# Eight scatters of a turn issued one by one behind the turn's matrix products, in the first graph layer

## The chip, the cores and the metric

The kernel runs on one core of a Trainium2 chip. The metric is the device time of one execution, in microseconds; lower is better. Times are given as the median of several executions, with the lowest and the highest beside it.

## The reference, cut to what matters

The program is a stack of four graph layers and four feed-forward layers over 32 graphs of 256 nodes with 128 features, all in float32. The change is in the first graph layer, which also prepares the routing of the first feed-forward layer:

```python
# layer 0, graph part, with h = layer norm of x
h1 = relu(bn1(conv1(h)));  h2 = bn2(conv17(h1));  x_conv = relu(h2 + h)
s = h @ w_se.T + b_se;     A = exp(-dist(s)) * mask
msg = relu(h @ w_msg.T + b_msg);  x_nmp = A @ msg
gi = [x_conv, x_nmp] @ w_ih.T + b_ih;  gh = h @ w_hh.T + b_hh
r = sigmoid(gi_r + gh_r);  z = sigmoid(gi_z + gh_z)
out = (1 - z) * tanh(gi_n + r * gh_n) + z * h;   x = x + out
# layer 0, feed-forward part: two of 16 experts for each row
logits = norm(x) @ gate_w + gate_b;  top_k(softmax(logits), 2)
y = sum over the two of gate * ((silu(row @ w1) * (row @ w2)) @ w3)
```

The reference computes every expert for every row; the kernel sorts the rows by expert first. Each normalised row is written twice, to a slot in the region of each of its two experts in a buffer in device memory called `sorted_rows`.

## The kernel before

**Turns.** The 8192 rows are worked in 16 turns of 512 rows (two graphs, four tiles of 128 rows). `every_turn` (line 38) writes turns 0, 1, 14 and 15 out and loops over the others in pairs. Each engine has its own program, whose order is written by hand; engines meet only at semaphores. `B[0]` to `B[7]` are the eight PSUM banks.

**TensorE in turn t** (lines 591 to 667), in this order, with the semaphore that each product raises: the first convolution (`c1_ps`), the distance features (`s_ps`), the messages (`msg_ps`), the ranks of turn t-2 for the router, convolution taps (line 607), the transposes of turn t-1's output (`out_ps`), the hidden state's product (`ghn_ps`, line 629), the distances (`dist_ps`, line 634), more taps with `shared_ps` and then `c2_ps` (line 642), the router's transposes of the normalised rows of turn t-1 (`hT_ps` of the route, line 1019), the transposes for turn t+1 (line 581), the neighbours' sum (`nmp_ps`, line 654), the router's logits of turn t-1 (`logits_ps`, line 1027), and the gate products (lines 661, 664, 667), of which the last three raise `r_ps`, `n_ps` and `z_ps`.

**The router's chain, for turn t-1, within turn t.** VectorE adds the residual and takes the row statistics (`vector_stats`, which ends with the variance on line 854, `var_ready`). GpSimd raises the variance to the power -0.5 (`pool_rstd`, line 966, `rstd_ready`). VectorE makes the shift (`vector_shift`, lines 859 and 861). ScalarE writes the normalised rows into `rows[par]` (`scalar_rows`, line 985, `h_ready`). TensorE transposes them (line 1019), ScalarE copies that out of PSUM (line 994), TensorE makes the logits (line 1027), and VectorE picks the two experts (lines 868 to 908). ScalarE's program has the copy of line 552 (`g_shared`) right behind the four copies of line 985; TensorE's line 654 waits for it. VectorE's normalisation of turn t+1 (line 185) is behind line 861.

**Places and scatters, for turn t-2, within turn t.** VectorE turns the ranks into slots (`vector_places`, line 940, `slots_ready`), ahead of the residual of turn t-1. GpSimd then issues eight scatters (`dispatch`, line 756): two experts times four tiles of 128 rows, each an indirect DMA of 128 rows of 528 bytes. There are two buffers of rows and slots, taken in turn; `vector_shift` waits until the scatters of a buffer have landed (two turns earlier) before it writes it again.

**GpSimd before** has nothing else in a turn: the power for t-1 first, then the eight scatters for t-2 in a row.

**SyncE** loads two 512 KB blocks of adjacency a turn, two turns ahead: the first once line 457 has used its buffer, the second after line 472. So turns 14 and 15 load nothing.

The same `Route` class serves two later layers; their GpSimd programs (lines 1560 to 1583 and 2990 to 3010) call `pool_dispatch`, as before.

Of the kernel before, what the change touches and what calls it, by code (L numbers as in the profile page):

```python
# [21 lines left out]
ALU = mybir.AluOpType  # L22
# [9 lines left out]
TT = TURN // P  # L32
# [5 lines left out]
def every_turn(eng, body, count=TURNS, begin=1):  # L38

    for t in range(begin + 1):  # L40
        body(t, t % 2, t == 0, False)
    with eng.Fori(begin + 1, count - 3, 2) as t:
        body(t, 0, False, False)
        body(t + 1, 1, False, False)
    body(count - 2, 0, False, False)
    body(count - 1, 1, False, True)
# [186 lines left out]
def wait_past(eng, sem, value):  # L233

    if not isinstance(value, int) or value > 0:
        eng.wait_ge(sem, value)


def counted(eng, value):

    return value if isinstance(value, int) else eng.to_reg(value)
# [9 lines left out]
def phase_gnn0(nc, c):  # L251
# [14 lines left out]
    with ExitStack() as ctx:  # L266
# [3 lines left out]
        def sem(name):  # L270
            return c.sem("g0_" + name)
# [38 lines left out]
        dist_ps, exp_ready, A_ready = sem("dist_ps"), sem("exp_ready"), sem("A_ready")  # L310
# [5 lines left out]
        c2_ps, xpre_ready, xconv_ready = sem("c2_ps"), sem("xpre_ready"), sem("xconv_ready")  # L316
        nmp_ps, nmp_ready = sem("nmp_ps"), sem("nmp_ready")
        ghn_ps, r_ps, z_ps, n_ps = sem("ghn_ps"), sem("r_ps"), sem("z_ps"), sem("n_ps")
# [5 lines left out]
        route = Route(nc, c, "ffn0", c.moe, ctx, B[2], B[2], B[2])  # L324

        with nc.Block() as block:
            @block.sync
            def _(sp):
                def load(t, par, first, last):
                    if not first and not (isinstance(t, int) and t == 1):  # L330
                        sp.wait_ge(A_ready, t - 1)
                    sp.dma_start(adj[par][:], c.adjT[t]).then_inc(adj_ready[par], 16)
                    if not first and not (isinstance(t, int) and t == 1):
                        sp.wait_ge(degrees_done, t - 1)
                    sp.dma_start(adj_rows[par][:], c.adj[t]).then_inc(adj_rows_ready[par], 16)
                    if isinstance(t, int) and t == 1:
                        nxt = c.order[1]
                        sp.dma_start(c.block[nxt], c.dram[nxt]).then_inc(c.w_ready[nxt], 16)
                every_turn(sp, load)

            @block.gpsimd
            def _(g):

                g.wait_ge(consts, 1)
                g.tensor_tensor(bnc[:, 6:8], bnc[:, 4:6], c.minus_half[:, 0:2], ALU.pow).then_inc(consts_pow, 1)
                route.pool_begin(g)

                def turn(t, par, first, last):
                    if first:
                        return  # L350
                    route.pool_rstd(g, t - 1)
                    if not (isinstance(t, int) and t == 1):
                        route.pool_dispatch(g, t - 2, par)
                every_turn(g, turn)
                route.pool_rstd(g, TURNS - 1)
                route.pool_dispatch(g, TURNS - 2, 0)
# [393 lines left out]
    r.dispatched = [c.dma_sem[name, "dispatched", i] for i in range(r.depth)]  # L750


def dispatch(eng, c, m, r, par):
    for k in range(m.top):
        for j in range(TT):
            eng.indirect_dma_start(c.sorted_rows, bass.IndirectOffsetOnAxis(r.slot[par][:, k, j:j + 1], 0),  # L756
                                   r.rows[par][:, j, :], None).then_inc(r.dispatched[par], 16)

# [6 lines left out]
class Route:  # L765
# [3 lines left out]
    def __init__(self, nc, c, name, r, ctx, rows_bank, logits_bank, rank_bank, in_phase=True):  # L769
        m, L = MOE[name], LAYOUT[name]  # L770
# [11 lines left out]
        def sem(n):  # L782
            return c.sem(f"{name}_r_{n}")
# [15 lines left out]
         self.logits_in, self.top_ready, self.shifted, self.first_eq, self.first_ready, self.hot_first, self.left_ready,  # L799
         self.second_top, self.second_eq, self.second_weighed, self.second_ready, self.hot_second, self.chosen_ready, self.exp_ready,  # L800
         self.den_ready, self.pair_sum, self.pair_eps, self.pair_inv, self.rank_ps, self.counted, self.used_ready,
         self.picked, self.slots_ready, self.inside_ready, self.kept_ready, self.routed) = (sem(n) for n in (
             "zeroed filled upto_ready merged squared joined rms var_ready "
             "rstd_ready shift_ready h_ready hT_ps hT_ready logits_ps "
             "logits_in top_ready shifted first_eq first_ready hot_first left_ready "
             "second_top second_eq second_weighed second_ready hot_second chosen_ready exp_ready "
             "den_ready pair_sum pair_eps pair_inv rank_ps counted used_ready "
             "picked slots_ready inside_ready kept_ready routed").split())
        self.scattered = r.dispatched

    def tiles_(self, ap):
        return ap[:, :, None].broadcast_to([P, TT, self.m.count])
# [155 lines left out]
    def pool_dispatch(self, g, t, par):  # L968
        done = counted(g, t + 1)
        g.wait_ge(self.zeroed, 2)  # L970
        g.wait_ge(self.slots_ready, done)
        g.wait_ge(self.h_ready, done)
        dispatch(g, self.c, self.m, self.r, par)

# [68 lines left out]
def moe_table(nc, c, name, m, w, r, nxt):  # L1045

    E, B = m.count, c.bank
    with ExitStack() as ctx:
# [19 lines left out]
        with nc.Block() as block:  # L1068
# [15 lines left out]
            @block.gpsimd  # L1084
            def _(g):
                dispatch(g, c, m, r, (TURNS - 1) % r.depth)
# [2496 lines left out]
```

## Time and profile before

| what | us |
|---|---|
| median of 3 executions (lowest to highest) | 3343.19 (3338.99 to 3350.63) |
| the profiled execution's own time | 3378.2 |
| its span, first to last instruction | 3376.4 |
| mean granted TensorE clock in it | 0.904 of full speed |
| busy in the span: PE, PEld, DVE, ACT, POOL | 2714.6, 2131.5, 2205.6, 1742.1, 872.7 |

PE is TensorE's matrix products and PEld its weight loads, DVE is VectorE, ACT is ScalarE, POOL is GpSimd. Work is named by line, engine, operation and tiles (out<-in). In a timeline each row has the start in the span, the time that it took, and in brackets how long its engine sat idle before it and what ended that. Starts of matrix products are recorded, their ends are modelled. "remote" stands where the semaphore moved at a time at which no instruction of the profile ended. The layer runs from the start to about 560 us; turn 2 starts near 92 us, turn 14 near 481.

### The profile page before, as it was taken

What the parts mean: (1) busy time and instruction counts of PE and PEld (TensorE: products, weight loads), DVE (VectorE), ACT (ScalarE), POOL (GpSimd) and SP (SyncE); (2) the same over time, 40 slices, a digit from 0 to 9 for tenths busy, and PEclk for the clock granted to TensorE, in tenths of its full rate; (3) what the DMA queues carried; (4) which work ended last, traced back from release to release, by engine and by line L of the source; (5) the groups of instructions that cost most, each with busy time, mean ns of one, the idle gap of its engine ahead of it and who ended that gap; (6) DMA issues with size and microseconds to landing.
All of it is one profiled execution on the core that took longest, in us unless ns stands there. A gap on an engine that the chain in (4) does not pass through costs nothing. (4 is left out here: it accounts for less than half of the span.)

```text
span 3376.4 us, 67489 instructions
## 1 busy us (share of the span) xinstructions
PE 2714.6 (80%) x19706; PEld 2131.5 (63%) x19706; DVE 2205.6 (65%) x6555; ACT 1742.1 (52%) x5034; POOL 872.7 (26%) x863
## 2 busy tenths in 40 slices
PE   5798995888677586578999998899987777669992
PEld 4566674877457585265777877566654444468882
DVE  5666664444467554767888885699986667644445
ACT  2233332444456453475656563677756666445553
POOL 0222332444425343230001010000001343434332
PEclk9899997999789798889999999899998888779996
DMA  5111111222332121320000000000010000022115
GB/s 195 42 46 48 57 45 47 67 63 65 117 123 76 50 58 47 126 79 1 1 1 0 0 1 10 26 19 25 19 34 37 21 24 20 26 59 56 53 53 165
DMA packets 142589, 169.06 MB, mean 50 GB/s; under 512 B 19920, under 2 KB 118224, under 8 KB 141776
## 3 DMA queue, kind: packets, MB, share of 16 engines
q1 hardware_dynamic: 116688, 118.67, 11.9%
q0 software_dynamic: 21504, 44.74, 3.9%
q10 hardware_dynamic: 4224, 3.59, 0.4%
q8 instruction: 79, 1.29, 0.2%
q14 instruction: 94, 0.77, 0.1%
HBM read 115.87 MB, written 51.05 MB: 49 GB/s over the span
## 5 line engine op out<-in xcount | busy, mean ns | idle before, releaser
L1375 PE MATMUL bank<-ffn_e_xT,ffn_e_mine 128*128 128x128 f32 x3360 | 462.8, 285 | 56.3 <-ACT ffn_e_mine L1309 24.4
L1233 POOL DMA_INDIRECT y_rows<-ffn_e_rows_out,ffn_e_scatter_at x352 | 339.0, 963 | 523.4 <-DVE ffn_e_rows_out L1261 331.6
L1375 PEld LDWEIGHTS bank<-ffn_e_xT,ffn_e_mine 128*128 128x128 f32 x3360 | 423.1, 199 | 68.0 <-issue 41.7
L756 POOL DMA_INDIRECT sorted_rows<-ffn_rows,ffn_slot x320 | 315.9, 987 | 231.2 <-issue 220.1
L1385 PE MATMUL bank<-ffn_e_mine,ffn_e_hid 128*128 128x128 f32 x1968 | 294.9, 283 | 39.1 <-DVE ffn_e_hid L1281 17.6
L1281 DVE TENSOR_TENSOR ffn_e_hid<-ffn_e_act,bank 128x256 f32<-128x256 f32 (+1 forms) x280 | 135.9, 485 | 276.3 <-ACT ffn_e_act L1335 245.1
L1309 ACT ACTIVATE ffn_e_mine<-constants 128x512 f32 (+1 forms) x352 | 250.9, 714 | 87.1 <-issue 64.4
L1385 PEld LDWEIGHTS bank<-ffn_e_mine,ffn_e_hid 128*128 128x128 f32 x1968 | 256.2, 196 | 55.9 <-DVE ffn_e_hid L1281 26.5
L2752 ACT ACTIVATE gnn_prob<-bank,gnn_low 128x256 f32<-128x256 f32 x512 | 203.0, 500 | 107.0 <-DVE gnn_low L2666 107.0
L1335 ACT ACTIVATE ffn_e_act<-bank 128x256 f32<-128x256 f32 (+1 forms) x280 | 120.8, 431 | 247.0 <-PE bank L1375 174.1
L1269 DVE TENSOR_SCALAR ffn_e_mine<-constants 128x256 f32 (+2 forms) x352 | 123.6, 354 | 119.6 <-PE bank L1385 73.0
L966 POOL TENSOR_TENSOR ffn_r_rstd<-ffn_r_var,minus_half 128x4 f32<-128x4 f32 x48 | 49.8, 1038 | 576.9 <-DVE ffn_r_var L854 405.7
L2666 DVE TENSOR_REDUCE gnn_low<-bank 128x2 f32<-128x512 f32 x256 | 158.9, 683 | 23.1 <-PE bank L2851 20.4
L2677 DVE SCALAR_TENSOR_TENSOR gnn_probT<-gnn_adj,bank 128x512 f32<-128x512 f32 x256 | 163.6, 680 | 7.5 <-PE bank L2863 4.2
L2276 ACT ACTIVATE bank<-bank,f_low 128x64 f32<-128x64 f32 x512 | 150.1, 308 | 14.0 <-DVE f_low L2073 13.9
L2863 PE MATMUL bank<-ident,gnn_prob 128*128 128x128 f32 x1024 | 141.9, 279 | 5.1 <-DVE gnn_probT L2677 4.7
L2863 PEld LDWEIGHTS bank<-ident,gnn_prob 128*128 128x128 f32 x1024 | 112.0, 141 | 39.7 <-ACT gnn_prob L2752 26.7
L3047 DVE TENSOR_REDUCE att_low<-bank 128x1 f32<-128x128 f32 (+1 forms) x256 | 75.8, 348 | 92.5 <-DMA g_adj<-in_adjT 72.3
L3266 PE MATMUL bank<-ident,att_prob 128*128 128x128 f32 x384 | 73.1, 304 | 59.5 <-ACT att_probT L3157 34.6
L2276 ACT ACTIVATION_READ_ACCUMULATOR bank<-bank,f_low 128x1 f32 x512 | 116.9, 228 | 0.0
L2650 POOL TENSOR_TENSOR X<-X,constants 128x512 f32 (+1 forms) x16 | 17.4, 1089 | 359.8 <-ACT gnn_h L2771 359.8
L3266 PEld LDWEIGHTS bank<-ident,att_prob 128*128 128x128 f32 x384 | 48.6, 154 | 97.4 <-ACT att_probT L3157 49.0
(515 smaller groups left out, 6552.1 us busy)
## 6 DMA issues: line engine op xcount, KB each, us to landing
g_adj<-in_adjT SPq DMA_DIRECT2D x48, 512.0 KB, 3.8
ffn_e_rows_in<-sorted_rows SPq DMA_DIRECT2D x346, 66.0 KB
ffn_c_y<-y_rows SPq DMA_DIRECT2D x80, 256.0 KB, 3.7
g_adj_rows<-in_adj SPq DMA_DIRECT2D x16, 512.0 KB
gnn_adj<-in_adjT SPq DMA_DIRECT2D x16, 512.0 KB, 3.8
constants<-in_ffn SPq DMA_DIRECT2D x1, 6281.0 KB, 22.1
y_rows<-ffn_e_rows_out,ffn_e_scatter_at POOLq DMA_INDIRECT x352
constants<-in_ffn SPq DMA_DIRECT2D x1, 5204.0 KB, 15.5
```

The lines of the kernel that those rows point to most:

```text
L756: eng.indirect_dma_start(c.sorted_rows, bass.IndirectOffsetOnAxis(r.slot[par][:, k, j:j + 1], 0), r.rows[par][:, j, :], None).then_inc(r.d ...
L1233: g.indirect_dma_start(c.y_rows, bass.IndirectOffsetOnAxis(scatter_at[par][:, k:k + 1], 0), rows_out[par][:, k, :], None).then_inc(scatter ...
L1269: v.tensor_scalar(mine3[place][:].rearrange("p (e c d) -> p e c d", e=1, c=NCH), w3[:, ds(e, 1), :, :], 1.0, None, ALU.mult).then_inc(seco ...
L1281: v.tensor_tensor(hid[k][:], act[k % 2][:], up, ALU.mult).then_inc(hid_ready, 1)
L1309: a.activation(mine1[place][:, None, :], w1[:, ds(e, 1), :], ACT.Copy).then_inc(first_copied, 1)
L1375: ins = pe.matmul(chunk(part, ch), chunk(weights[:, i * HALF:(i + 1) * HALF], ch), x, start=True, stop=True)
L1385: ins = pe.matmul(B[6 + par][:, k * D:(k + 1) * D], chunk(hid[k][:], ch), chunk(mine3[k][:], ch), start=(ch == 0), stop=(ch == NCH - 1))
L2276: ins = a.activation(lg, lg, ACT.Exp, bias=low[k % 2][:, hd:hd + 1], scale=-1.0, accum_out=sm[k % 2][:, hd:hd + 1])
L2666: v.tensor_reduce(low[q % 2][:, j, :], S[j].rearrange("p (q k) -> p q k", q=2), AX.X, ALU.min).then_inc(low_ready, 1)
L2677: v.scalar_tensor_tensor(probT[q % 2][:, j, :, :], adj[par][:, 2 * g:2 * g + 2, :], 1e-6, T_BANK[j % 2].rearrange("p (k q) -> p k q", k=2) ...
L2752: ins = a.activation(prob[q % 2][:, j, qt, :], S[j][:, qt * NODES:qt * NODES + NODES], ACT.Exp, bias=low[q % 2][:, j, qt:qt + 1], scale=-1.0)
L2863: ins = pe.transpose(T_BANK[j % 2][:, col:col + P], prob[q % 2][:, j, qt, kt * P:kt * P + P], c.ident[:])
```

## The change

Only the first graph layer's GpSimd program is changed. Turn 1 does its power as before. From turn 2 on, the eight scatters of turn t-2 are issued one by one: the first once the slots are there, the second behind `ghn_ps`, the third behind `dist_ps`; then comes the power for turn t-1; the fourth is behind `c2_ps`, the fifth behind `nmp_ps`, the sixth behind the router's `logits_ps`, the seventh behind `r_ps` and the eighth behind `z_ps`. Ahead of each scatter GpSimd adds two columns of one element a partition (`tick`) and raises a new semaphore `paced`; the next scatter's `tick` waits for the one before. The scatters of turn 14, after the last turn, and all other layers are as before. Two semaphores that only a layer with a capacity uses are made only there.

```diff
--- before.py
+++ after.py
@@ -348,9 +348,26 @@
                 def turn(t, par, first, last):
                     if first:
                         return
+                    if isinstance(t, int) and t == 1:
+                        g.wait_ge(route.zeroed, 2)
+                        route.pool_rstd(g, 0)
+                        return
+                    route.pool_few(g, t - 2, par, (0,))
+                    g.wait_ge(ghn_ps, t + 1)
+                    route.pool_few(g, t - 2, par, (1,))
+                    g.wait_ge(dist_ps, t + 1)
+                    route.pool_few(g, t - 2, par, (2,))
                     route.pool_rstd(g, t - 1)
-                    if not (isinstance(t, int) and t == 1):
-                        route.pool_dispatch(g, t - 2, par)
+                    g.wait_ge(c2_ps, t + 1)
+                    route.pool_few(g, t - 2, par, (3,))
+                    g.wait_ge(nmp_ps, t + 1)
+                    route.pool_few(g, t - 2, par, (4,))
+                    g.wait_ge(route.logits_ps, t)
+                    route.pool_few(g, t - 2, par, (5,))
+                    g.wait_ge(r_ps, t + 1)
+                    route.pool_few(g, t - 2, par, (6,))
+                    g.wait_ge(z_ps, t + 1)
+                    route.pool_few(g, t - 2, par, (7,))
                 every_turn(g, turn)
                 route.pool_rstd(g, TURNS - 1)
                 route.pool_dispatch(g, TURNS - 2, 0)
@@ -750,9 +767,11 @@
     r.dispatched = [c.dma_sem[name, "dispatched", i] for i in range(r.depth)]
 
 
-def dispatch(eng, c, m, r, par):
+def dispatch(eng, c, m, r, par, mine=range(2 * TT)):
     for k in range(m.top):
         for j in range(TT):
+            if k * TT + j not in mine:
+                continue
             eng.indirect_dma_start(c.sorted_rows, bass.IndirectOffsetOnAxis(r.slot[par][:, k, j:j + 1], 0),
                                    r.rows[par][:, j, :], None).then_inc(r.dispatched[par], 16)
 
@@ -799,14 +818,15 @@
          self.logits_in, self.top_ready, self.shifted, self.first_eq, self.first_ready, self.hot_first, self.left_ready,
          self.second_top, self.second_eq, self.second_weighed, self.second_ready, self.hot_second, self.chosen_ready, self.exp_ready,
          self.den_ready, self.pair_sum, self.pair_eps, self.pair_inv, self.rank_ps, self.counted, self.used_ready,
-         self.picked, self.slots_ready, self.inside_ready, self.kept_ready, self.routed) = (sem(n) for n in (
+         self.picked, self.slots_ready, self.routed) = (sem(n) for n in (
              "zeroed filled upto_ready merged squared joined rms var_ready "
              "rstd_ready shift_ready h_ready hT_ps hT_ready logits_ps "
              "logits_in top_ready shifted first_eq first_ready hot_first left_ready "
              "second_top second_eq second_weighed second_ready hot_second chosen_ready exp_ready "
              "den_ready pair_sum pair_eps pair_inv rank_ps counted used_ready "
-             "picked slots_ready inside_ready kept_ready routed").split())
-        self.scattered = r.dispatched
+             "picked slots_ready routed").split())
+        self.inside_ready, self.kept_ready = (sem(n) if m.capacity else None for n in ("inside_ready", "kept_ready"))
+        self.scattered, self.paced = r.dispatched, sem("paced") if m.top > 1 else None
 
     def tiles_(self, ap):
         return ap[:, :, None].broadcast_to([P, TT, self.m.count])
@@ -971,6 +991,16 @@
         g.wait_ge(self.slots_ready, done)
         g.wait_ge(self.h_ready, done)
         dispatch(g, self.c, self.m, self.r, par)
+
+    def pool_few(self, g, t, par, mine):
+
+        if 0 in mine:
+            done = counted(g, t + 1)
+            g.wait_ge(self.slots_ready, done)
+            g.wait_ge(self.h_ready, done)
+        wait_past(g, self.paced, 2 * TT * t + mine[0])
+        g.tensor_tensor(self.c.tick[:, 5:6], self.c.tick[:, 0:1], self.c.tick[:, 0:1], ALU.add).then_inc(self.paced, 1)
+        dispatch(g, self.c, self.m, self.r, par, mine)
```

## Rows read from the trace of the kernel before

**Rows 1.** Stretches: length; busy PE, PEld, DVE, ACT, POOL; granted clock, DMA share, GB/s.
```profile
60.30:92.20 31.90, 28.22 (x145) 21.69 (x144) 23.00 (x76) 10.93 (x22) 1.02 (x1) 0.89 0.11 33
139.40:481.30 341.90, 311.67 (x1651) 222.68 (x1651) 220.54 (x661) 120.04 (x231) 96.57 (x99) 0.95 0.17 51
481.30:534.50 53.20, 52.26 (x296) 38.78 (x295) 37.38 (x114) 21.16 (x42) 17.55 (x18) 1.00 0.07 22
...
321.20:324.60 3.40, 2.90 (x4) 0.84 (x3) 1.28 (x6) 1.25 (x2) 0.17 (x1) 0.50 0.06 20
```

**Rows 2.** Timeline of turn 8: GpSimd, and the work that its power releases.
```profile
310.27 1.04 POOL L966 TENSOR_TENSOR ffn_r_rstd<-ffn_r_var,minus_half 128x4 f32<-128x4 f32 x1 [21.64 <-DVE ffn_r_var L854]
...
311.51 1.03 POOL L756 DMA_INDIRECT sorted_rows<-ffn_rows,ffn_slot  x1 [0.20 <-issue]
...
311.93 0.15 DVE L861 SCALAR_TENSOR_TENSOR ffn_r_shift<-ffn_r_mean,ffn_r_rstd 128x4 f32<-128x4 f32 x1
...
312.24 1.65 ACT L985 ACTIVATE ffn_rows<-X,ffn_r_shift,ffn_r_rstd 128x128 f32 x4 [2.98 <-DVE ffn_r_shift L861]
...
320.42 0.95 POOL L756 DMA_INDIRECT sorted_rows<-ffn_rows,ffn_slot  x1 [0.30 <-issue]
```

**Rows 3.** Timeline of turn 8: products, and the first work that waits for each.
```profile
314.28 0.60 PE L1019 MATMUL bank<-ident,ffn_rows 128*128 128x128 f32 x4
...
314.71 0.60 PE L581 MATMUL bank<-ident,g_h 128*128 128x128 f32 x4
...
315.15 1.89 PE L654 MATMUL bank<-g_A,g_msg 128*128 128x256 f32 x8
...
318.75 0.60 ACT L994 ACTIVATE ffn_r_hT<-bank 128x512 f32<-128x512 f32 x1 [4.49 <-remote]
...
319.39 1.06 PE L1027 MATMUL bank<-constants,ffn_r_hT 128*128 128x16 f32 x8 [2.35 <-ACT ffn_r_hT L994]
320.18 0.60 ACT L514 ACTIVATE g_hT<-bank 128x512 f32<-128x512 f32 x1 [0.84 <-remote]
...
323.05 0.60 ACT L558 ACTIVATE g_nmp<-bank 128x512 f32<-128x512 f32 x1 [2.28 <-remote]
323.15 0.23 DVE L868 TENSOR_TENSOR ffn_r_left<-bank,constants 128x64 f32<-128x64 f32 x1 [6.08 <-remote]
```

**Rows 4.** Timeline of turn 1, in which nothing is scattered.
```profile
81.60 0.60 PE L1019 MATMUL bank<-ident,ffn_rows 128*128 128x128 f32 x4
...
82.24 0.60 ACT L994 ACTIVATE ffn_r_hT<-bank 128x512 f32<-128x512 f32 x1 [2.12 <-PE bank L1019]
```

**Rows 5.** Timeline of turn 14, in which SyncE loads nothing.
```profile
498.39 1.89 PE L654 MATMUL bank<-g_A,g_msg 128*128 128x256 f32 x8
...
501.93 0.60 ACT L558 ACTIVATE g_nmp<-bank 128x512 f32<-128x512 f32 x1 [2.26 <-remote]
...
502.73 2.74 PE L664 MATMUL bank<-g_nmp,constants 128*128 128x512 f32 x6
```

**Rows 6.** Waits of the whole span whose release has no instruction at its time ("remote").
```profile
DVE ffn_r_left L868 <- remote: 76.2, 14, 6.1
...
ACT att_probT L3157 <- remote: 60.4, 20, 6.6
```

**Rows 7.** Timeline of turn 8: when the slots and the early products are there.
```profile
306.26 1.89 PE L634 MATMUL bank<-g_of_n,g_of_m 128*128 128x256 f32 x8
...
306.64 0.29 DVE L940 TENSOR_REDUCE ffn_slot<-ffn_r_places 128x8 uint32<-128x128 f32 x1
...
313.80 0.46 ACT L552 ACTIVATE g_shared<-bank,g_bnc 128x256 f32<-128x256 f32 x1
```

**Rows 8.** GpSimd by form: line, shapes, count, busy us and mean ns of one.
```profile
L2012 POOL TENSOR_TENSOR f_rstdy<-f_ve,minus_half 128x1 f32<-128x1 f32 x16 | 8.8, 550 | 240.0 <-DVE f_ve L2176 240.0
...
L961 POOL CAST ffn_upto<-ffn_upto 128x128 bf16<-128x128 f32 x3 | 0.9, 287 | 0.0
...
L3577 POOL MEMSET const-float32-0.0<- 128x1 f32 x1 | 0.1, 98 | 0.3 <-issue 0.3
```


## The prediction

> **What bounds the layer now.** I read the stretches first. Turns 3 to 13 take 341.90 us, 31.08 each, and have 311.67 / 11 = 28.33 of TensorE in them; turns 14 and 15 take 53.20, 26.60 each, with 26.13 of TensorE [rows 1]. So TensorE is the layer's bound, but in the middle turns it stands still for 2.7 us a turn and works longer, at a mean clock of 0.95 where the last two have 1.00. Both kinds of turn have the same eight scatters. What turns 14 and 15 lack is SyncE's loads (DMA share 0.07 for 0.17).
>
> The timeline of a middle turn shows the idle time. The router's transposes begin at 314.28 and are over by 314.88, but ScalarE's copy of them starts at 318.75, after 4.49 us of idle time ended by "remote"; TensorE then waits 2.35 us for that copy before the logits. The three other readers of products in the same stretch are late too: the copy of line 514 at 320.18 for a product of 314.71, line 558 at 323.05 for one that ended at 317.04, line 868 at 323.15 for one that ended at 320.45 [rows 3]. All of this is in the shadow of eight scatters in a row, 311.51 to 321.37 [rows 2]. In turn 1, where nothing is scattered though SyncE loads, the copy starts at 82.24, 0.04 after its product's end [rows 4]. So while scatters run, and most of all while they run beside loads, TensorE's semaphores reach their waiters 2.7 to 6 us late. The standstill also costs clock: from 321.20 to 324.60 TensorE was granted 0.50, its 1.2 GHz level [rows 1]. In turn 14 line 558 was late as well (501.93 for a product that ended at 500.28), but line 664 behind it went on at 502.73 with no idle time before it [rows 5]: about 1.6 us of lateness is covered by TensorE's other products. Later layers have the same kind of wait (60.4 us on line 3157) [rows 6]; they are not touched.
>
> **Part 1: the burst is taken apart.** Removed is the middle turns' excess over turns 14 and 15, 31.08 - 26.60 = 4.48 us, eleven times: 49 us. Turn 2 has the same wait but a start of its own, so I count one more turn at 3: 52 in all. It ends with the excess gone if an increment beside a single scatter is late by no more than the 1.6 us that is covered. The bounds are 0 late (a turn as the last two) and as late as now (nothing gained). I take the first, because the fourth scatter now starts behind `c2_ps`, with only itself beside the load, the fifth waits for `nmp_ps`, and so each scatter begins after an increment has arrived and never more than one is in flight with the next. What is late next is small: the eighth scatter starts behind `z_ps`, and the next turn's first convolution, whose reader is on the chain, comes 0.9 us later. Bounded by 0 and one scatter with its gap, 1.26 us [rows 2], I take 0.3 a turn, 14 turns: 4 us, ends 0 and 18.
>
> **Part 2: the power comes later.** Now it starts at 310.27, as soon as the variance is there [rows 2]. After the change three scatters stand ahead of it on GpSimd. The slots are ready at 306.64 + 0.29 = 306.93, and the distances end at 308.15, before GpSimd could ask for them [rows 7]. Each scatter takes 0.96 us, the first of a row 1.03, with 0.30 between two and 0.20 behind a GpSimd operation [rows 2]. The addition has no row. Its bounds are a one-column fill, 0.10, and a one-column power, 0.55; I take 0.3, the nearest in kind being the cast at 0.29 [rows 8]. So: 306.93 + 0.15 for the release, + (0.3 + 0.2 + 1.03), + 2 x (0.3 + 0.3 + 0.2 + 0.96), + 0.1 = 312.2. The power is 1.9 us later.
>
> Who waits for it: the shift (311.93), behind it on VectorE the normalisation of the next turn, and the four row copies, over at 313.89 [rows 2]; behind these on ScalarE the copy of line 552, over at 314.26 [rows 7], and on TensorE the transposes of line 1019, which begin at 314.28 with no idle time noted before them [rows 3], 0.39 behind the rows' end. A release took 0.16 (312.08 to 312.24 [rows 2]), so about 0.25 of the 1.9 is slack and the rest is TensorE's: 1.65 us a turn. Line 654 needs line 552's copy and is pushed by the same amount, not more. It hits all 14 turns from 2 to 15: 23 us. With the addition and its gaps hidden in the gap between scatters, the power would be 0.7 late and the cost 0.4 a turn, 6 us; with 0.55 and wider gaps 2.8 late and 2.5 a turn, 36 us.
>
> The Trainium skill ("SBUF — State Buffer", section "SBUF: two separate sides") says that a vector operation in a two-port mode locks GpSimd out of the port with which it writes descriptors; the first three scatters move under line 194's copy of X, which could be such a one. The scatters' durations here, 0.95 to 1.03 beside all kinds of vector work, show no such lengthening [rows 2], and the sum leaves it out.
>
> **Part 3: the rest.** Seven more waits a turn stand in GpSimd's queue, and only the power and scatters are behind them; those of `r_ps` and `z_ps` end the turn and the next turn's slots come some 8 us later. The eight additions are 8 x 0.3 = 2.4 us of an engine busy 8.8 in 31 (96.57 / 11) [rows 1]. The last scatter of a buffer lands a few us into the next turn, 10 us before line 859 writes a buffer again. The semaphores moved cost nothing.
>
> **Sum.** In the profiled execution: 3378.2 - 52 + 4 + 23 = 3353, 25 us less. That execution is itself 35.0 above the median of the runs, so part of the lateness may be the profile's own. The late increments are worth 52 us here and 60 in the later layer [rows 6]; if all 35 lay in them, they would be 31% smaller in a timed run, and the gain 36 - 27 = 9 us. Between 25 and 9 I take 18: 3343.2 - 18 = 3325.
>
> **Rivals.**
> *The stall goes, and shows in the timed runs* (the above): 3325, its own range 3301 to 3334. For it: the lateness stands in every middle turn, and 112 us of it cannot all be the profile's when the profile costs 35. Chance 0.46.
> *The stall is only moved.* One scatter beside a load already makes TensorE's increments late, `nmp_ps` or the logits lag as before, and half of the 52 comes back, 26, against costs of 27: 3343 to 3345. For it: the last two turns lack the loads, so the profile never shows a lone scatter beside a load; against it: the lateness grows along the burst. The same time comes out if the waits are over before GpSimd reaches them, so that the scatters stay bunched. Chance 0.24.
> *Slower: the power's delay without the gain.* If the lateness is nearly all the profile's, timed turns already run like turn 14, and what is left is TensorE's 1.65 us behind the power, 14 times, and 0.3 behind the eighth scatter: 3343 + 23 to 27 = 3366 to 3370. It decides once less than half of the 52 us is in timed runs. For it: copies came 1.43 us apart after four transposes of line 581 (318.75 to 320.18) and twice that, 2.87, after line 654's eight records (320.18 to 323.05) [rows 3], as if every instruction had something to hand over, not only those with a semaphore. The Trainium skill ("NOTIFIC — the notification-queue block", section "7.1 Overflow: three behaviours, one of which stalls the engine") says that the block that collects trace records holds its producers back when its inner queues fill. Against it: 35 us is too little for all. Chance 0.30.
>
> **How the numbers follow.** About 0.3%, 10 us, is what a measurement of this kernel can tell from no change. Faster by more than that is the first case, 0.46; within it the second, 0.24; slower the third, 0.30. The forecast is the first case's time. The range goes from its best end, 52 removed with 6 to 11 paid, 3301, to 3366, the third case's lower end; the rest of that case is left out.
>
> **What would show it.** In the profile after: the power at 1 to 2.5 us after the variance in turns 2 to 15, with three scatters before it; TensorE idle by 1.2 to 2 us ahead of line 1019, ended by line 985; the "remote" waits of lines 994, 558 and 868 gone or under 2 us; turns 3 to 13 at 28 to 29 us and turns 14 and 15 at 28 to 28.5, longer than before. I am wrong on the gain if lines 558 and 868 still start 3 us late, wrong on the cost if line 1019 does not wait, and wrong on the profile's share if profiled and timed executions move by different amounts.

## The result and the profile after

The changed kernel takes 3308.18 us in the median of 4 runs (3300.98 to 3310.47), the kernel before 3344.07 us (4 runs, 3338.99 to 3350.63). The ratio is 0.9888, with a 95% interval from 0.9864 to 0.9912, so 36 us are gone. The ratios here and below are estimated from the single runs, and lie within 0.001 of the quotient of the medians. The profiled execution of the changed kernel took 3306.19 us with a span of 3304.4, which is 72 us less than that of before.

The stretches of the layer on the core; the columns are those of [rows 1]. The first is turns 3 to 13, the second turns 14 and 15:

```profile
134.80:434.60 299.80, 291.99 (x1651) 218.27 (x1651) 223.39 (x661) 119.30 (x231) 117.66 (x188) 1.00 0.19 58
434.60:487.70 53.10, 52.23 (x296) 38.91 (x295) 39.03 (x117) 21.23 (x41) 21.59 (x35) 1.00 0.07 21
```

Turns 3 to 13 take 299.80 / 11 = 27.25 us where they took 31.08 [rows 1]. TensorE is busy in 97% of that time for 91%, and its granted clock is 1.00 for 0.95, the upper of its two levels throughout. Turns 14 and 15 take 53.10 for 53.20. The middle turns now nearly look like the last two, as part 1 of the prediction had it, and SyncE's loads run beside them at a slightly higher share, 0.19 for 0.17, as the same bytes come in less time.

The waits of the whole span that end in "remote" (total, times, longest), in the changed kernel:

```profile
ACT att_probT L3187 <- remote: 59.9, 20, 6.4
...
ACT ffn_e_act L1365 <- remote: 21.1, 8, 3.3
```

and in the kernel before, the four largest beside those of [rows 6]:

```profile
ACT ffn_e_act L1335 <- remote: 67.6, 20, 6.4
...
ACT ffn_r_hT L994 <- remote: 44.6, 11, 4.5
...
ACT g_nmp L558 <- remote: 31.9, 14, 2.3
...
ACT g_hT L514 <- remote: 11.6, 12, 1.6
```

The first layer's four readers of products (lines 994, 558, 514 and 868, now 1024, 575, 531 and 888) are gone from the list; they stood there with 44.6 + 31.9 + 11.6 + 76.2 us. So is a fifth, line 476 with 5.1 us, which waits for `c2_ps`. The last attention layer's wait (line 3157, now 3187), which the change doesn't touch, is as it was: 59.9 for 60.4 us. The wait in the expert stages (line 1335, now 1365) fell from 67.6 to 21.1 us, though nothing was changed there. It goes with the 25 us by which the two profiled executions are further apart (72) than the layer's own end moved, 534.5 - 487.7 = 46.8. The experiments show that this second part is no work of the change.

The timeline of one middle turn of the changed kernel, GpSimd and what hangs on it (start, duration, then in brackets the idle time before and what ended it):

```profile
307.38 0.18 POOL L1002 TENSOR_TENSOR tick<-tick 128x1 f32<-128x1 f32 x1 [7.23 <-DVE ffn_slot L960]
...
308.04 1.08 POOL L775 DMA_INDIRECT sorted_rows<-ffn_rows,ffn_slot  x1 [0.48 <-issue]
...
309.51 0.99 POOL L775 DMA_INDIRECT sorted_rows<-ffn_rows,ffn_slot  x1 [0.16 <-issue]
...
310.36 0.17 DVE L874 TENSOR_SCALAR ffn_r_var<-ffn_r_spread 128x4 f32<-128x4 f32 x1
...
310.53 0.20 POOL L1002 TENSOR_TENSOR tick<-tick 128x1 f32<-128x1 f32 x1
310.89 0.99 POOL L775 DMA_INDIRECT sorted_rows<-ffn_rows,ffn_slot  x1 [0.16 <-issue]
...
311.91 1.04 POOL L986 TENSOR_TENSOR ffn_r_rstd<-ffn_r_var,minus_half 128x4 f32<-128x4 f32 x1
...
312.49 2.22 PE L624 MATMUL bank<-g_uv_lo,g_taps_hi 128*128 128x256 f32 x17
...
312.99 0.16 DVE L881 SCALAR_TENSOR_TENSOR ffn_r_shift<-ffn_r_mean,ffn_r_rstd 128x4 f32<-128x4 f32 x1 [0.52 <-POOL ffn_r_rstd L986]
...
313.28 1.66 ACT L1015 ACTIVATE ffn_rows<-X,ffn_r_shift,ffn_r_rstd 128x128 f32 x4 [3.75 <-DVE ffn_r_shift L881]
...
315.00 0.66 PE L1049 MATMUL bank<-ident,ffn_rows 128*128 128x128 f32 x4 [0.28 <-ACT ffn_rows L1015]
...
315.69 0.60 ACT L1024 ACTIVATE ffn_r_hT<-bank 128x512 f32<-128x512 f32 x1 [0.39 <-PE bank L1049]
...
317.66 0.96 PE L1057 MATMUL bank<-constants,ffn_r_hT 128*128 128x16 f32 x8
...
318.65 0.22 DVE L888 TENSOR_TENSOR ffn_r_left<-bank,constants 128x64 f32<-128x64 f32 x1 [0.56 <-PE bank L1057]
```

Three things are to be seen. The copy of line 1024 starts at 315.69, 0.03 after the transposes end (315.00 + 0.66); before, it was 3.87 late (318.75 for 314.88) [rows 3]. Line 888 starts at 318.65 for a product that ends at 318.62, 0.03 behind it and not 2.70 [rows 3]. And the power starts at 311.91, 1.38 after the variance (310.36 + 0.17), with three scatters before it; the transposes of line 1049 now wait for the row copies of line 1015, by 0.28 us.

### The profile page after: what moved, and what is told of

The parts are those of the page before. It is cut to its first block and busy times, and to the rows that moved or that the text cites. A ratio compares the mean times of both kernels' runs of the same rounds, so it can differ in the third digit from the quotient of the medians.

```text
span 3304.4 us, 67716 instructions
## 1 busy us (share of the span) xinstructions
PE 2681.5 (81%) x19706; PEld 2125.6 (64%) x19706; DVE 2209.8 (67%) x6555; ACT 1746.3 (53%) x5034; POOL 901.4 (27%) x975
## 6 DMA issues: line engine op xcount, KB each, us to landing
constants<-in_ffn SPq DMA_DIRECT2D x1, 6281.0 KB, 22.1
```

## The experiments

There are twelve experiments, each compared with runs of the kernel before on the same chip. Set 1 ran on one chip, set 2 and set 3 on a second, all but the ticked row of set 3, which ran on a third. Which chip the result was measured on isn't recorded. The kernel before did not take the same time on them: 3075.75 us on the first (23 runs, 3072.06 to 3082.35), 3369.76 and 3368.25 on the second, 3367.07 on the third (7, 6 and 7 runs, 3362.54 to 3377.0 in all), and 3344.07 with the result. So times are only compared on one chip. In this part an increment is the step by which a product raises its semaphore, and the lateness is the time from the end of a product to the start of the instruction that reads it.

### Set 1: a chip without late increments

**The kernel before, unchanged**, was run to learn how much two executions of one program differ.

> The kernel before, unchanged, to see how far one profiled execution lies from the timed ones and whether the middle turns of the first layer always take 31 us. If the late increments are of every execution: ratio 1.00, and its profile has middle turns near 31 us again with the 'remote' waits on lines 994, 558 and 868. If the profiled execution of before was an unusual one (3378 against 3344): its middle turns will be shorter, 28 to 29.5 us, and the span near 3342. The rival, that the trace itself makes them late: turns of 31 us again and a profiled execution 30 us or more above the timed runs.

Measured: 3075.88 us, ratio 0.9999 (0.9989 to 1.0009). Its turns 3 to 13, and its own row of eight scatters, of which the first two are shown (timeline):

```profile
136.00:430.40 294.40, 289.73 (x1651) 218.28 (x1651) 220.64 (x661) 119.08 (x232) 96.56 (x99) 1.00 0.21 59
```

```profile
309.85 1.03 POOL L756 DMA_INDIRECT sorted_rows<-ffn_rows,ffn_slot  x1 [0.20 <-issue]
...
311.19 0.96 POOL L756 DMA_INDIRECT sorted_rows<-ffn_rows,ffn_slot  x1 [0.30 <-issue]
...
312.72 0.60 PE L1019 MATMUL bank<-ident,ffn_rows 128*128 128x128 f32 x4
...
313.36 0.60 ACT L994 ACTIVATE ffn_r_hT<-bank 128x512 f32<-128x512 f32 x1 [0.70 <-PE bank L1019]
...
313.60 1.89 PE L654 MATMUL bank<-g_A,g_msg 128*128 128x256 f32 x8
...
315.52 0.60 ACT L558 ACTIVATE g_nmp<-bank 128x512 f32<-128x512 f32 x1 [1.08 <-PE bank L654]
```

The program is the same, the scatters stand 1.26 us apart behind the first (1.34) as in [rows 2], the DMA share is 0.21, and yet line 994 starts 0.04 after its product and line 558 0.03 after its own. Not one wait in the whole span ends in "remote". A middle turn takes 294.4 / 11 = 26.76 us. So the lateness is no property of the program alone: on this chip, in this one set of runs, it is absent, and the kernel before is 268 us faster here than with the result. This chip serves as the control without lateness.

**Bunched**: the waits on the five later products are left out of the changed kernel.

```diff
-                    g.wait_ge(c2_ps, t + 1)
                     route.pool_few(g, t - 2, par, (3,))
-                    g.wait_ge(nmp_ps, t + 1)
                     route.pool_few(g, t - 2, par, (4,))
...
```

> The change without the five waits behind c2, nmp, logits, r and z: three scatters, the power, then five scatters in a row, 1.4 us apart with the addition between them. If it is the burst beside the loads that makes TensorE's increments late: the lateness comes back in part (five scatters instead of eight, further apart), middle turns 28.5 to 30.5 us, and the time is 3325 to 3345 against 3308 for the change. If any break in the row of eight is enough: as the change, 3308, turns 27.2.

Measured: 3084.37 us, ratio 1.0035 (1.0022 to 1.0048).

**The power ahead of the third scatter**, the rest as in the change.

```diff
+                    route.pool_rstd(g, t - 1)
                     g.wait_ge(dist_ps, t + 1)
                     route.pool_few(g, t - 2, par, (2,))
-                    route.pool_rstd(g, t - 1)
```

> The change with the power ahead of the third scatter instead of behind it. The power then starts about 1.4 us earlier, right at the variance; TensorE's wait of 0.27 us ahead of the router's transposes goes. If the late power costs what the profile of the changed kernel shows, 0.6 us a turn (27.24 against 26.6 in the last turns before) at most: 3308 minus 4 to 9 = 3299 to 3304. If the power's delay is hidden: 3308.

Measured: 3075.87 us, ratio 1.0006 (0.9997 to 1.0014).

**Two additions** ahead of each scatter in place of one, the rest as in the change.

```diff
+        g.tensor_tensor(self.c.tick[:, 4:5], self.c.tick[:, 0:1], self.c.tick[:, 0:1], ALU.add)
         g.tensor_tensor(self.c.tick[:, 5:6], self.c.tick[:, 0:1], self.c.tick[:, 0:1], ALU.add).then_inc(self.paced, 1)
```

> The change with a second one-element addition ahead of every scatter. Each is 0.20 us, so the power comes 0.6 us later or more and TensorE waits as much longer ahead of the router's transposes: 14 x 0.6 = 8 us, 3316. If the late power is covered: 3308.

Measured: 3086.47 us, ratio 1.0036 (1.0022 to 1.0049).

What follows from the four: where there is no lateness there is nothing to win, and the late power is a loss of its own, 9 us between the medians (ratio 1.0035) with three scatters and their additions ahead of it, nothing that can be measured with two. By the traces turns 3 to 13 take 27.23 us in "bunched", and 26.75 in the kernel before and with the power ahead of the third scatter. Two additions were expected to make a turn 0.6 us longer and the kernel 8 us slower. The turns grew by 0.3, to 27.55; the scatters ahead of the power stand 1.51 us apart for 1.38, so a second addition adds 0.13 and not 0.20, and the 2 us between the medians of the two kernels (3084.37 and 3086.47) are within what their own runs differ by. The change itself wasn't timed on this chip; "bunched" has the same three scatters ahead of the power. This is the case of the prediction's third rival, the delay without the gain, at a smaller cost than it gave.

### Set 2: a chip with late increments, and more loads

**The change, unchanged.**

> The change itself, unaltered, on the chip of these experiments. If the late increments of TensorE are what the change removes, and this chip shows none of them in the kernel before (turns of 26.7 us, time 3076): nothing is left to gain, only the late power costs; turns of 27.2 us as in the kernel 'bunched', 11 x 0.5 = 6 us and a little more in the other turns, ratio 1.002 to 1.004, 3082 to 3088. If the gain of 36 us has another cause than those increments: ratio about 0.99. If the chip is one that shows them (before near 3344): ratio 0.989.

Measured: 3324.35 us against 3369.76, ratio 0.9873 (0.9856 to 0.9889). The waits that end in "remote":

```profile
ACT ffn_e_act L1365 <- remote: 61.4, 19, 6.0
ACT att_probT L3187 <- remote: 60.8, 19, 6.6
```

The layer has none left, and its turns 3 to 13 take 27.25 us again. But line 1365 waits 61.4 us, nearly as much as it did before the change (67.6), where the result's trace had 21.1. So the fall to 21.1 belongs to that execution or chip, and the change's own part is the 47 us in the layer. In time it is 3369.76 - 3324.35 = 45.4 us here, and the two agree.

**The kernel before, and the changed kernel, each with three more loads a turn**: SyncE copies three more blocks of 512 KB each turn into device memory that nobody reads.

```diff
+                    if not first:
+                        sp.wait_ge(extra_in, 16 * EXTRA * t)
+                    for one in extra:
+                        sp.dma_start(one, c.adjT[t]).then_inc(extra_in, 16)
```

> The kernel before (eight scatters in a row behind the power), with three more copies of the turn's 512 KB adjacency block, into unused device memory, issued by SyncE beside the first load of each turn. If more load traffic beside the scatters is what makes TensorE's increments late: 'remote' waits on lines 994, 558 and 868 come up on this chip too and middle turns grow from 26.7 to 28 or more. If the lateness has nothing to do with the amount of DMA traffic: turns stay at 26.7 to 27, apart from a later load of the rows' block.

> The change with the same three more copies a turn. If traffic makes the increments late and taking the row of eight apart cures it: turns 27.2 to 27.5, shorter than in the kernel with the row and the same copies. If traffic has no part: 0.5 us a turn longer than that kernel, as without the copies.

Measured, in two executions of each: the row of eight with more loads 3392.72 us, ratio 1.0072 (1.0052 to 1.0092); the changed kernel with more loads 3323.8, ratio 0.9868 (0.9848 to 0.9887). Turns 3 to 13 of each, first the row of eight:

```profile
139.80:501.70 361.90, 319.35 (x1651) 228.10 (x1650) 221.19 (x661) 119.70 (x232) 96.54 (x99) 0.92 0.30 96
```

```profile
134.80:434.60 299.80, 292.23 (x1652) 218.35 (x1651) 223.19 (x660) 119.12 (x232) 117.26 (x188) 1.00 0.36 116
```

With the row of eight, a DMA share of 0.30 for 0.17 [rows 1] makes a middle turn 361.9 / 11 = 32.9 us, 1.8 more, at a clock of 0.92. The router's copy (line 994 of the kernel before) starts on average 4.5 us after its product in turns 3 to 13, and 6.7 at most, where the trace of the kernel before has 3.2 and 3.9. With the scatters apart, a share of 0.36 costs nothing at all: 27.25 us and a clock of 1.00. So loads make the lateness worse, but they don't make it alone. The second rival, that one scatter beside a load is enough, falls.

### Set 3: what in the change does it

**Bunched** once more, on a chip with late increments.

> The kernel 'bunched' once more: three scatters, the power, then five in a row 1.4 us apart, with no waits on products behind the power. So far it was only seen on a chip on which no increment of TensorE came late. If this chip shows them (the kernel before near 3345 to 3370): by the theory that a row of scatters beside a load makes them late, five in a row bring part of the lateness back, middle turns 28.5 to 30.5, ratio 0.990 to 1.000 where the change has 0.987; by the rival that any break in the row is enough, turns of 27.2 and 0.987. If the chip shows none (near 3076): 1.0035 again.

Measured: 3327.9 us, ratio 0.9883 (0.9866 to 0.9901). Some rows of a middle turn:

```profile
289.95 0.98 POOL L770 DMA_INDIRECT sorted_rows<-ffn_rows,ffn_slot  x1 [0.16 <-issue]
...
291.31 0.96 PE L1052 MATMUL bank<-constants,ffn_r_hT 128*128 128x16 f32 x8
291.32 0.98 POOL L770 DMA_INDIRECT sorted_rows<-ffn_rows,ffn_slot  x1 [0.16 <-issue]
...
292.84 0.22 DVE L883 TENSOR_TENSOR ffn_r_left<-bank,constants 128x64 f32<-128x64 f32 x1 [1.06 <-PE bank L1052]
```

The turns of 28.5 to 30.5 us that a row of five was expected to bring did not come. Without the waits on products turns 3 to 15 take 27.1 us. Behind the power five scatters follow each other some 1.4 us apart (289.95 to 291.32 is 1.37). Part of the lateness is back all the same: line 883 is late by 0.57 in this turn (292.84 for 292.27) and by up to 1.37 in others, and the turn hides it.

**Spaced**: the power is first, as before the change; then the eight scatters come with no wait on a product, but behind a power of eight columns each.

```diff
-                        route.pool_dispatch(g, t - 2, par)
+                        for k in range(8):
+                            route.pool_few(g, t - 2, par, (k,), 8)
```

> The order of before (the power first, then the eight scatters with no wait on any product), but with a power of eight columns (1.65 us) ahead of each scatter, which puts them about 3 us apart. If what counts is the distance between scatters: no late increments, middle turns 26.7 to 27, ratio 0.985 to 0.987 on a chip with late increments, 1.000 on one without. If they have to stand behind the products, so that no increment is under way with a scatter: late increments by 1 to 3 us remain on lines 994, 558 or 868, turns 27.5 to 29, ratio 0.988 to 0.995.

Measured: 3315.83 us, ratio 0.984 (0.9823 to 0.9858). The scatters are 2.93 us apart, with a power of 1.6 to 1.7 us between two of them:

```profile
286.58 1.03 POOL L761 DMA_INDIRECT sorted_rows<-ffn_rows,ffn_slot  x1 [0.20 <-issue]
...
287.41 0.96 PE L1046 MATMUL bank<-constants,ffn_r_hT 128*128 128x16 f32 x8
...
288.41 0.23 DVE L874 TENSOR_TENSOR ffn_r_left<-bank,constants 128x64 f32<-128x64 f32 x1 [0.81 <-PE bank L1046]
...
289.52 1.03 POOL L761 DMA_INDIRECT sorted_rows<-ffn_rows,ffn_slot  x1 [0.19 <-issue]
```

Turns 3 to 15 take 26.7 us, and no increment is late: line 874, between two scatters, starts 0.04 after its product (288.41 for 287.41 + 0.96). The products that the change chose as gates play no part.

**Ticked row**, on a third chip with its own runs of the kernel before: the same with one addition of one column ahead of each scatter in place of the eight-column power. It tells the addition from the other thing that "bunched" still had, a row parted by the power.

```diff
-                            route.pool_few(g, t - 2, par, (k,), 8)
+                            route.pool_few(g, t - 2, par, (k,))
```

> The power first as in the kernel before, then all eight scatters of the turn in one unbroken row, a one-column addition of 0.20 us ahead of each, no wait on a product. Scatters start about 1.37 us apart instead of 1.26, and nothing else stands between them. Theory A (the operation between two scatters, or the 0.1 us that it adds to their distance, is enough): no wait ended by 'remote' in the layer, middle turns at 26.75 us as with the 8-column powers, ratio to the kernel before 0.984 to 0.986 on a chip with late increments. Theory B (the row has to be broken: the earlier run without product waits was cured because the power parted three scatters from five): eight in a row at 1.37 us still make TensorE's increments late, middle turns at 28.5 to 31 us, lines 994 and 868 still end waits by 'remote', ratio 0.992 to 1.003. On a chip where the kernel before runs near 3076 both give 26.75 us and a ratio of 0.999 to 1.002, and the run tells nothing between them.

Measured: 3319.47 us against 3367.07, ratio 0.9855 (0.9839 to 0.9872). In time this is what theory A gives. A middle turn:

```profile
286.58 0.60 PE L1038 MATMUL bank<-ident,ffn_rows 128*128 128x128 f32 x4
...
287.02 0.60 PE L584 MATMUL bank<-ident,g_h 128*128 128x128 f32 x4
...
287.60 0.60 ACT L1013 ACTIVATE ffn_r_hT<-bank 128x512 f32<-128x512 f32 x1 [1.05 <-PE bank L1038]
...
288.26 0.98 POOL L761 DMA_INDIRECT sorted_rows<-ffn_rows,ffn_slot  x1 [0.16 <-issue]
...
289.07 0.60 ACT L517 ACTIVATE g_hT<-bank 128x512 f32<-128x512 f32 x1 [0.88 <-PE bank L584]
289.18 0.96 PE L1046 MATMUL bank<-constants,ffn_r_hT 128*128 128x16 f32 x8
...
289.63 0.98 POOL L761 DMA_INDIRECT sorted_rows<-ffn_rows,ffn_slot  x1 [0.16 <-issue]
...
291.37 0.23 DVE L874 TENSOR_TENSOR ffn_r_left<-bank,constants 128x64 f32<-128x64 f32 x1 [2.00 <-PE bank L1046]
```

The increments are still late, in this turn by 0.42 us (line 1013), 1.45 (line 517, for 287.62) and 1.23 (line 874 for 290.14), and in other turns by more. Theory A had expected no wait of the layer to end in "remote", but two lines have such waits, as theory B had it:

```profile
DVE ffn_r_left L874 <- remote: 21.4, 7, 4.8
...
ACT ffn_r_hT L1013 <- remote: 7.3, 3, 2.5
```

But the turn hides nearly all of it: turns 3 to 15 take 349.2 / 13 = 26.9 us. The lateness of three readers over turns 3 to 13, each from its timelines (mean, and in brackets the longest, in us):

| kernel | scatters start apart | router's copy | neighbours' copy | expert choice | a turn |
|---|---|---|---|---|---|
| before, eight in a row | 1.26 | 3.2 (3.9) | 5.4 (6.0) | 3.1 (5.2) | 31.08 |
| ticked row, eight in a row | 1.37 | 1.1 (1.9) | 1.4 (2.0) | 1.8 (3.5) | 26.92 |
| bunched, five in a row behind the power | 1.37 to 1.58 | 0.4 (0.5) | 0.6 (1.4) | 1.0 (1.4) | 27.23 |
| spaced | 2.93 | 0.03 (0.04) | 0.04 (0.04) | 0.04 (0.04) | 26.75 |

(The readers are lines 994, 558 and 868 of the kernel before.) An addition between two scatters, and 1.37 us for 1.26 from one to the next, brings the mean lateness from 3.1 to 5.4 us down to 1.1 to 1.8, and the turn to within 0.2 us of the shortest; a distance of 2.93 takes away the rest. At nearly the same distance five in a row leave less of it than eight.

**The power ahead of the third scatter**, on this chip.

> The kernel 'power_third' (the change, with the power ahead of the third scatter) once more. On a chip with late increments: the gain of the change and no late power, middle turns 26.7 to 26.8 against 27.2, so 14 x 0.45 = 6 us under the change: ratio 0.985 to 0.986 where the change has 0.987. If moving the third scatter behind the power brings it beside the load and makes increments late: turns over 27.5, ratio over 0.988. On a chip without: 1.000 again.

Measured: 3318.33 us, ratio 0.9854 (0.9836 to 0.9871). The start of the turns' last activation, of turns 2 to 15, in this kernel and in the change:

```profile
L583 ACT ACTIVATE bank<-bank,g_rz_half x14: 662/662/665, 134.0 to 481.3; 128x512 f32<-128x512 f32 x14
```

```profile
L583 ACT ACTIVATE bank<-bank,g_rz_half x14: 663/664/666, 134.8 to 487.7; 128x512 f32<-128x512 f32 x14
```

Thirteen turns take 481.3 - 134.0 = 347.3 us, 26.72 each, where the change has 487.7 - 134.8 = 352.9, 27.15 each. All of it is in turns 3 to 13, 26.75 for 27.25; turn 14 takes 26.7 to 26.8 and turn 15 26.3 in both.

**The same, and the last attention layer's row spaced too**, with a power of two columns ahead of each of its scatters.

```diff
-                        route.pool_dispatch(g, t - 2, par)
+                        g.wait_ge(route.zeroed, 2)
+                        for k in range(8):
+                            route.pool_few(g, t - 2, par, (k,), 2)
```

> 'power_third', and in the last attention layer, which has eight scatters in a row in 14 turns too, a power of two columns (0.73 us) ahead of each scatter, so about 2 us apart instead of 1.26. On a chip with late increments: the waits on line 3187 (3157 of before; 60 us in the profile of before) shrink, and its turns of 25 to 26 us fall by 1 to 3 us: 15 to 40 us under power_third, ratio 0.974 to 0.981. If 2 us apart is still a row: no change against power_third. On a chip without: 1.000 to 1.002.

Measured: 3265.29 us, ratio 0.9691 (0.9674 to 0.9709). The waits of that layer's copies, first with its row of eight as it was, then spaced:

```profile
ACT att_probT L3187 <- remote: 60.8, 20, 6.6
```

```profile
ACT att_probT L3192 <- PE bank L3301: 20.1, 18, 1.4
```

The 60.8 us are gone and the time is 3318.33 - 3265.29 = 53.0 us lower, more than the 15 to 40 expected. In the last attention layer, too, the row of scatters causes the lateness. This version beats both kernels, on a chip of this kind.

## Why the prediction was right, and where it wasn't

The forecast was 3325 us with a range of 3301 to 3366, and its case, that the stall goes and that this shows in the timed runs, is what happened. The measured 3308 lies within the range, 17 us under the forecast. Two terms of the sum were wrong, and both made the gain too small: the cost by some 20 us and the last step by 7 (both below). The range was wide enough to hold that. With both put right the same sum gives 3343.2 - 45 = 3298, 10 us below the result, so the number's closeness is worth less than the mechanism's.

**Part 1, the burst taken apart: the size was right.** The middle turns lost 31.08 - 27.25 = 3.83 us each, and with part 2's cost of 0.5 added back that is 4.3, against the 4.48 predicted. The reason given for it was half right. Scatters that are apart don't make increments late, but not because each waits for a product. "Bunched" wins the same without the waits, and "spaced" and "ticked row" have shorter turns than the change with the power first. What counts is that something stands between two scatters and keeps them a little apart; the runs don't part the operation from the distance it makes. The other half held: lateness of 1 to 2 us, as in the ticked row, is nearly covered by TensorE's other products, as the 1.6 us of the prediction had it.

**Part 2, the late power: the delay was somewhat too long, its cost far too high.** The power was expected 1.9 us later. Measured against line 607's last taps, which start at 312.22 before and, as line 624, at 312.49 now, it stands 1.37 us later (312.22 - 310.27 = 1.95 ahead before, 312.49 - 311.91 = 0.58 now). The additions take 0.18 to 0.20 us rather than 0.3, and start 0.03 behind a scatter (310.53 for 309.51 + 0.99, timeline above) rather than 0.3. The cost was expected at 1.65 us in each of 14 turns, and it was 27.25 - 26.75 = 0.5 in turns 3 to 13, the second number from the kernel with the power ahead of the third scatter, and nothing in turns 14 and 15. In time, on one chip, 3324.35 - 3318.33 is 6 us, not 23. The step that failed is "about 0.25 of the 1.9 is slack". It counted the slack between the row copies and TensorE only. VectorE had some of its own: before, the shift of line 861 started at 311.93 although the power was over at 310.27 + 1.04 = 311.31 [rows 2], because VectorE was busy with line 457 until 311.95 (timeline of the kernel before):

```profile
310.67 1.28 DVE L457 TENSOR_TENSOR g_A<-bank,g_adj 128x512 f32<-128x512 f32 x2
```

That is 0.6 of slack. In the changed kernel the shift starts 0.04 after the power's end, behind 0.52 of idle time. 0.25 + 0.6 leaves 1.37 - 0.85 = 0.5, the cost measured. Turn 14 bears this out (timeline of the changed kernel):

```profile
474.44 1.04 POOL L986 TENSOR_TENSOR ffn_r_rstd<-ffn_r_var,minus_half 128x4 f32<-128x4 f32 x1
...
475.54 2.22 PE L624 MATMUL bank<-g_uv_lo,g_taps_hi 128*128 128x256 f32 x17
...
477.60 0.60 PE L1049 MATMUL bank<-ident,ffn_rows 128*128 128x128 f32 x4
```

There the power stands 475.54 - 474.44 = 1.10 ahead of the taps, where it stood 495.46 - 493.56 = 1.90 ahead in turn 14 of the kernel before. That is 0.80 later, within the slack of 0.85, and the transposes of line 1049 have no idle time before them. Three signs that the prediction named did not come: TensorE idle by 1.2 to 2 us ahead of line 1019 (it is 0.28), turns 3 to 13 at 28 to 29 us (27.25), and turns 14 and 15 longer than before at 28 to 28.5 (53.10 / 2 = 26.55, as before). The port that the sum left out did not show: the first scatter, beside line 194's copy (307.83 to 308.26), took 1.08 us, 0.1 more than the next.

GpSimd's 112 additions in the layer take 0.198 us each and 22.1 in all, of an engine with room.

**Part 3, the rest** cost nothing, as said, and of the 0.3 us a turn put on the eighth scatter nothing was found: all increments of the changed layer arrive at once.

**The sum's last step failed.** It took the 35 us between the profiled execution of before and its median for the profile's own work and cut the gain from 25 to 18. The changed kernel's profiled execution lies among its other runs (3306.19 between 3300.98 and 3310.47), and "kernel before, unchanged" agrees with its set too. On the chips of sets 2 and 3 the kernel before took 3362.54 to 3377.0 us in all of 20 runs, close to the profiled 3378.2. The difference that I gave to recording is of the size of the difference between chips. Whether the profiled execution of before came from such a chip isn't recorded. With part 2 at 6 to 7 us and the eighth scatter at 0, the sum in the profile is 52 - 7 = 45, which is what set 2 measured (45.4), and near the 46.8 in the layer's end. With the result it was 36 (3344.07 - 3308.18); why it was 9 less there isn't settled, as no trace of the kernel before at the level of 3344 exists.

**The rivals.** "The stall is only moved" fell with the extra loads of set 2. "Slower" named the right mechanism with the wrong cause: it decides where the lateness is absent, and that went with the chip. Set 1 shows it on "bunched", at 1.0035 instead of the 1.007 to 1.008 that its 23 to 27 us would have made. Recording alone does not make the lateness: the profiled executions of set 1 were recorded too, and had none.

**What stays open.** What in the chip makes TensorE's increments late while GpSimd issues a row of scatters, and why one chip doesn't do it. In the kernel before the copies came 1.43 us apart after four transposes [rows 3], as if each instruction had something to hand over. That would fit the Trainium skill, "NOTIFIC — the notification-queue block", section "7.1 Overflow: three behaviours, one of which stalls the engine", by which that block's inner queues hold producers back rather than lose a record. No run here can tell, since every execution is listed with a span and a clock, and nothing here shows what one does when nothing is recorded. Nor can the runs part the chip from its state at that hour, since the chip without lateness was used in one set only. Nor was it tried whether a longer distance with an idle GpSimd does the same as one with an operation in it.

## What to carry to other kernels

Where readers of TensorE's products start microseconds late with a wait that no instruction ends, look at what GpSimd issues in those microseconds: a row of scatters 1.26 us apart did it here, and one small operation between two of them brought the lateness down so far that the turn hid it. Keep what others wait for, here the power, ahead of the scatters, and before pricing a delay look at whether the waiter's own engine was busy at the time the delayed value used to arrive. Time a kernel and its change on one chip, and if possible on two, since one program took 3076 us on one chip and 3370 on another and a version of this change with the same late power is 1.2% faster on the second and 0.35% slower on the first.

## What the hardware showed that was not expected

Two chips differ, for one program, by nearly 10%: 3075.75 against 3369.76 us, while runs of it on one chip agree within 0.5%. Where it is slow the kernel before shows the waits ended by "remote", in this layer, in the expert stages and in the last attention layer, and a mean clock of 0.904 to 0.909 for 0.924 to 0.929. The lateness depends steeply on the distance of the scatters, or on the operation that makes it: means of 3.1 to 5.4 us at 1.26 and of 1.1 to 1.8 at 1.37, in a trace of each (table in set 3). And GpSimd starts a scatter 0.16 us behind an addition but 0.48 behind one that followed a wait (timeline of the changed kernel, 308.04), where two scatters in a row have 0.30 between them. The 0.48 is seen in the looped turns only: in turn 14, which is written out, the first scatter starts at 470.66, 0.16 behind its addition, though that had waited 7.55 us.
